# A fused field-interaction kernel on one core: later loads of F, a fifth output slot, and last-tile rows at 128 batches

## The chip, the cores and the metric

The kernel runs on one core of a Trainium2 chip. The metric is the device time of one launch in microseconds (us). Everything is float32 at the interface; the projections run on operands split into a high and a low part.

## The reference

```python
# F: (2048, 64, 128), W: (64, 64, 128), K_w and Q_w: (128, 128)
Kf  = einsum('bjd,ed->bje', F, K_w)
S   = einsum('bid,bjd->bij', F, Kf)
out = einsum('bij,ijd->bid', S, W) + einsum('bid,ed->bie', F, Q_w)
```

For every batch b a 64 x 64 table of scores S is made from F and its K projection. Each row i of that table is multiplied with its own 64 x 128 matrix W[i], and the Q projection of F is added.

## The kernel before, in words

The 2048 batches go in 16 tiles of 128 (`TILES`), a tile in 8 units of 16 batches (`UNITS`), and a tile's projection in 16 chunks of 512 columns (`CHUNKS`). F lies transposed in HBM. It comes in by pairs of units, 1 MB a load, into the six slots of `f_ring` (line 50), on the DMA queue of the sync engine (SP). One round of the steady state works on two tiles at once, and TensorE (PE) goes through it in this order (lines 514 to 518):

1. `scores_tile(t)` (L444, matmuls at L440): for each unit of tile t, 16 products of `kf` with F, into the unit's PSUM bank; `s_done` counts units. ACT and DVE copy the scores out in pairs of units into `s_t` (L217 to 219 and L314 to 316; `copy_s`). The banks are free of the earlier row sums when `out_done` says so (L454).
2. `project(t + 1)` (L406): for each chunk a K product (`k_done`) and a Q product (`q_done`), three matmuls each (L387 to 389): high by high, high by low, low by high. ACT copies both results out of PSUM (L199, L208). The high part `f_hi` of a unit is made by ACT (L194) or by DVE (L306), the low part `f_lo` by DVE (L292), both in three slots that come free with `q_done`. The first chunks each wait for the copies of the scores.
3. `rows_tile(t)` (L470, matmuls at L466): for each of 8 blocks, 4 values of m by 2 halves, W[i] against the scores of all 128 batches of the tile. Each block fills two banks; `o_done` counts blocks. DVE adds the Q part into an output slot of `o_sb` (L325, `sum_out`), counted by `out_done`, and SP stores the slot, 512 KB (L149, `store`). `sum_out` waits until the store from that slot four sums ago is done (L323). Blocks 4 to 7 wait for `out_done`, because they use the banks of blocks 0 to 3.

A float32 matmul stands as two instructions in the trace, each with its own weight load (LDWEIGHTS, shown as PEld). The split (fp32r) projection matmuls are one instruction each.

The order on SP is written out by hand (L160 to L172). In round t it is: stores 4 to 6 of tile t-1; the load of the first pair (`load_next(t, 0)`, L139) once two units of scores are made; store 7 of tile t-1; the loads of pairs 1, 2 and 3, once four, six and eight units of scores are made; and stores 0 to 3 of tile t. The pair that `load_next(t, j)` asks for has number 4t + j + 6 and overwrites the pair that the scores of units 2j and 2j+1 read last. So load 0 brings units 4 and 5 of tile t+1, load 1 its units 6 and 7, and loads 2 and 3 bring units 0 to 3 of tile t+2. With unit numbers counted over all tiles, DVE splits units 4, 6 and 8 (`both_f`) when the Q products of 4, 8 and 12 chunks of the projection are made (the wait at L305), and ACT splits 3, 5, 7 and 9 after chunks 1, 5, 9 and 13, and 10 at the round's end (L253 to L262).

The last tile has no projection behind its scores. Its rows go in another way (`rows_last`, L483): first for the batches of units 0 to 3 (part 0), then for those of units 4 to 7 (part 1), each in 4 blocks of 8 values of m with 64 batches (L504). DVE adds them with `sum_last` (L330, L338). So part 0 can begin while the scores of units 4 to 7 are still being copied.

Of the kernel before, what the change touches and what calls it, by code (L numbers as in the profile page):

```python
# [31 lines left out]
OBUF = 4  # L32
# [5 lines left out]
def build(nc, f_0, f_t, k_t, q_t, w, out):  # L38
    with ExitStack() as ctx:
# [21 lines left out]
        k_raw = sbuf("k_raw", [D, D])  # L61
        q_raw = sbuf("q_raw", [D, D])
# [4 lines left out]
        zeros = sbuf("zeros", [D, BANK], F32R)  # L67
# [19 lines left out]
        o_done, out_done = sem("o_done"), sem("out_done")  # L87
# [34 lines left out]

        lower, upper = slice(0, N), slice(N, P)
# [4 lines left out]
        def _(sp):  # L128
# [10 lines left out]
            def load_next(t, j):  # L139

                p = t * PAIRS + j + RING
                if p < TILES * PAIRS:
                    sp.wait_ge(s_done, t * UNITS + 2 * j + 2)
                    load_f(p)
# [15 lines left out]
            for t in range(TILES):  # L160
                if t >= 1:
                    for k in range(4, 7):
                        store(t - 1, k)
                load_next(t, 0)
                if t >= 1:
                    store(t - 1, 7)
                for j in range(1, PAIRS):
                    load_next(t, j)
                for k in range(4):
                    store(t, k)  # L170
            for k in range(4, UNITS):
                store(TILES - 1, k)  # L172
            for n in range(OBUF):
                sp.wait_ge(o_stored[n], 16 * (TILES * UNITS // OBUF))

        @block.scalar
        def _(act):
# [43 lines left out]
            act.dma_start(k_raw[:, :], k_t).then_inc(k_in, 16)  # L221
            act.dma_start(f_half_cols(1), f_0[0, :, half_cols(1)]).then_inc(f_half[1], 16)
            act.dma_start(q_raw[:, :], q_t).then_inc(q_in, 16)
            act.wait_ge(k_in, 16)
            nc.scalar.activation(k_hi[:, :], k_raw[:, :], COPY).then_inc(khi_done, 1)
# [3 lines left out]
            nc.scalar.activation(q_hi[:, :], q_raw[:, :], COPY).then_inc(qhi_done, 1)  # L229
# [33 lines left out]
            copy_s(TILES - 1, 1)  # L263
            copy_s(TILES - 1, 3)

        @block.vector
        def _(dve):
# [15 lines left out]
            def both_first(c):  # L283

                dve.wait_ge(f_first[c], 16)
                wait(dve, q_done, 2 * (c // 2 - SPLIT) + 2)
                nc.vector.tensor_copy(f_hi[:, c // 2 % SPLIT, piece_cols(c)], f_cols(c)).then_inc(fhi_dve, 1)
                dve.wait_ge(fhi_dve, c // 2)
                low_piece(c)
# [28 lines left out]
            def sum_out(t, k):  # L318
# [4 lines left out]
                wait(dve, o_stored[n % OBUF], n // OBUF * 16)  # L323
# [6 lines left out]
            def sum_last(half, k):  # L330

                n = (TILES - 1) * UNITS + half * 4 + k
                dve.wait_ge(o_done, n + 1)
                if half == 0 and k == 0:
                    dve.wait_ge(q_copied, TILES * CHUNKS)
                dve.wait_ge(o_stored[n % OBUF], n // OBUF * 16)
                bank = 2 * k % 8
                nc.vector.tensor_tensor(  # L338
                    o_sb[:, n % OBUF, :, :].rearrange("d s (x b) -> d s x b", b=KP * 4),
                    ps[:, bank:bank + 2, :].rearrange("d s (x b) -> d s x b", b=KP * 4),  # L340
                    q_out[:, (TILES - 1) % 2, :, :].rearrange("d (s m) (h b) -> d s (m h) b", s=2, h=2)[
                        :, :, k * 4 * IR:(k + 1) * 4 * IR, half * KP * 4:(half + 1) * KP * 4],
                    ALU.add).then_inc(out_done, 1)

            nc.vector.memset(zeros[:, :].bitcast(F32), 0.0).then_inc(zeros_done, 1)  # L345
            dve.wait_ge(khi_done, 1)
            nc.vector.tensor_tensor(k_lo[:, :], k_raw[:, :], k_hi[:, :].bitcast(F32),
# [4 lines left out]
            nc.vector.tensor_tensor(q_lo[:, :], q_raw[:, :], q_hi[:, :].bitcast(F32),  # L352
# [12 lines left out]
            for t in range(TILES):  # L365
# [11 lines left out]
                if t < TILES - 1:  # L377
                    for k in range(UNITS):
                        sum_out(t, k)
            for half in range(2):  # L380
                for k in range(4):
                    sum_last(half, k)

        @block.tensor
        def _(pe):
# [84 lines left out]
            def rows_tile(t):  # L470

                if t == 0:
                    pe.wait_ge(w_in, 16)
                for k in range(UNITS):
                    if k < 4:
# [3 lines left out]
                    else:  # L479
                        pe.wait_ge(out_done, t * UNITS + k - 3)  # L480
                    row_block(t, k)

            def rows_last(part):  # L483

                t = TILES - 1
                for k in range(4):
                    if part == 0:

                        pe.wait_ge(s_copied_act if k % 2 else s_copied, t * 2 + k // 2 + 1)
                        if k == 0:  # L490

                            pe.wait_ge(s_copied_act, t * 2 + 1)
                    else:
                        pe.wait_ge(out_done, t * UNITS + k + 1)
                    bank = 2 * k % 8
                    for x in range(2 * IR):
                        m = k * 2 * IR + x
                        for s in range(2):
                            half = slice(s * N, (s + 1) * N)
                            cols = s_t[half, m, :].rearrange("p (h b) -> p h b", h=2)[  # L500
# [49 lines left out]
```

## Time and profile before

| what | us |
|---|---|
| median of 3 runs | 623.38 |
| the runs | 621.13, 623.38, 625.32 |
| the profiled execution, its own time | 620.9 |
| its span, from the first to the last instruction | 619.1 |
| PE busy in the span | 606.5 (98%) |
| DVE busy | 403.9 |
| ACT busy | 402.0 |
| granted TensorE clock, mean | 0.995 |

The span is what the rows below are measured in. The other 1.8 us of the execution's own time lie around the span. In the rows, "PE" is the matmul, "PEld" its weight load, and "SPq" the sync engine as it issues DMAs. "Issue" as a releaser stands for idle time in which the engine waited for nothing that the profile shows.

### The profile page before, as it was taken

What the parts mean: (1) busy time and instruction counts of PE and PEld (TensorE: products, weight loads), DVE (VectorE), ACT (ScalarE), POOL (GpSimd) and SP (SyncE); (2) the same over time, 40 slices, a digit from 0 to 9 for tenths busy, and PEclk for the clock granted to TensorE, in tenths of its full rate; (3) what the DMA queues carried; (4) which work ended last, traced back from release to release, by engine and by line L of the source; (5) the groups of instructions that cost most, each with busy time, mean ns of one, the idle gap of its engine ahead of it and who ended that gap; (6) DMA issues with size and microseconds to landing.
All of it is one profiled execution on the core that took longest, in us unless ns stands there. A gap on an engine that the chain in (4) does not pass through costs nothing.

```text
span 619.1 us, 17442 instructions
## 1 busy us (share of the span) xinstructions
PE 606.5 (98%) x7822; PEld 535.9 (87%) x7822; DVE 403.9 (65%) x411; ACT 402.0 (65%) x695; POOL 0.2 (0%) x4
## 2 busy tenths in 40 slices
PE   9999999999999999899999999999989999999996
PEld 7888989889898988789889898898978889898896
DVE  6556758567595666657567686675946659476485
ACT  7887493866929387393874938669276592947720
POOL 0000000000000000000000000000000000000000
PEclk9999999999999999999999999999989999999999
DMA  8560937729185591935909367291852918646066
GB/s 327 233 266 35 372 140 262 284 105 373 68 299 247 199 343 48 373 130 210 336 34 357 156 245 300 103 369 76 309 236 98 375 74 292 255 163 247 4 271 274
DMA packets 29306, 137.57 MB, mean 222 GB/s; under 512 B 3248, under 2 KB 4016, under 8 KB 21168
## 3 DMA queue, kind: packets, MB, share of 16 engines
q1 hardware_dynamic: 28800, 136.20, 57.3%
q8 instruction: 62, 1.02, 0.6%
q10 hardware_dynamic: 432, 0.26, 0.1%
q14 instruction: 12, 0.10, 0.1%
HBM read 69.34 MB, written 67.11 MB: 220 GB/s over the span
## 4 chain that ended last, share of the span: by engine, by line
PE 94%; DMA 2%; DVE 1%; issue 1%; ACT 0%; DVEq 0%
PE ps L440 20%; PE ps L387 19%; PE ps L389 19%; PE ps L388 19%; PE ps L466 15%; PE ps L504 2%; DMA out<-o_sb 2%; DVE o_sb L325 1%; PE ps L511 1%; DVE o_sb L338 0%; ACT s_t L219 0%; ACT s_t L217 0%; DVE zeros L345 0%; ACT s_t L218 0%; DVEq L91 0%
## 5 line engine op out<-in xcount | busy, mean ns | idle before, releaser
L292 DVE TENSOR_TENSOR f_lo<-f_ring,f_hi 128x1024 fp32r<-128x1024 f32 x124 | 151.8, 1224 | 163.5 <-ACT f_hi L194 161.9
L208 ACT ACTIVATE q_out<-ps 128x512 f32<-128x512 f32 x256 | 156.7, 612 | 7.5 <-PE ps L389 0.3
L325 DVE TENSOR_TENSOR o_sb<-ps,q_out 128x1024 f32<-128x1024 f32 x120 | 140.2, 1219 | 32.5 <-PE ps L466 20.7
L199 ACT ACTIVATE kf<-ps 128x512 f32<-128x512 f32 x256 | 155.6, 608 | 7.8 <-PE ps L389 4.3
L217 ACT ACTIVATE s_t<-ps 128x512 f32<-128x512 f32 x32 | 19.1, 598 | 180.7 <-PE ps L440 180.7
L440 PE MATMUL ps<-f_ring,kf 128*64 128x64 f32 x4096 | 125.0, 223 | 1.7 <-issue 1.4
L440 PEld LDWEIGHTS ps<-f_ring,kf 128*64 128x64 f32 x4096 | 121.8, 138 | 5.0 <-issue 2.3
L466 PEld LDWEIGHTS ps<-s_t,w_sb 64*128 64x128 f32 x1920 | 108.4, 188 | 5.3 <-issue 5.3
L466 PE MATMUL ps<-s_t,w_sb 64*128 64x128 f32 x1920 | 111.2, 274 | 0.0
L387 PE MATMUL ps<-f_hi,k_hi 128*128 128x512 f32 (+1 forms) x258 | 102.0, 395 | 2.7 <-issue 2.7
L389 PE MATMUL ps<-f_hi,k_lo 128*128 128x512 f32 (+1 forms) x258 | 100.5, 390 | 1.9 <-issue 1.9
L388 PE MATMUL ps<-f_lo,k_hi 128*128 128x512 f32 (+1 forms) x258 | 100.5, 389 | 0.0
L387 PE MATMUL ps<-f_hi,q_hi 128*128 128x512 f32 x256 | 100.2, 391 | 0.0
L389 PE MATMUL ps<-f_hi,q_lo 128*128 128x512 f32 x256 | 99.9, 390 | 0.0
L388 PE MATMUL ps<-f_lo,q_hi 128*128 128x512 f32 x256 | 99.9, 390 | 0.0
L194 ACT ACTIVATE f_hi<-f_ring 128x1024 fp32r<-128x1024 f32 x77 | 82.0, 1064 | 0.0
L388 PEld LDWEIGHTS ps<-f_lo,k_hi 128*128 128x128 f32 x258 | 48.7, 189 | 12.5 <-issue 2.9
L387 PEld LDWEIGHTS ps<-f_hi,q_hi 128*128 128x128 f32 x256 | 48.3, 189 | 12.3 <-issue 2.1
L387 PEld LDWEIGHTS ps<-f_hi,k_hi 128*128 128x128 f32 x258 | 48.7, 189 | 10.6
L389 PEld LDWEIGHTS ps<-f_hi,k_lo 128*128 128x128 f32 x258 | 48.6, 189 | 10.1
L388 PEld LDWEIGHTS ps<-f_lo,q_hi 128*128 128x128 f32 x256 | 48.3, 189 | 10.1
L389 PEld LDWEIGHTS ps<-f_hi,q_lo 128*128 128x128 f32 x256 | 48.2, 188 | 10.2
(26 smaller groups left out, 195.3 us busy)
## 6 DMA issues: line engine op xcount, KB each, us to landing
out<-o_sb SPq DMA_DIRECT2D x128, 512.0 KB, 4.4
f_ring<-f_t SPq DMA_DIRECT2D x62, 1024.0 KB, 10.5
w_sb<-w SPq DMA_DIRECT2D x1, 2048.0 KB, 18.3
f_ring<-f SPq DMA_DIRECT2D x6, 256.0 KB, 4.7
f_ring<-f SPq DMA_DIRECT2D x3, 128.0 KB, 2.6
f_ring<-f ACTq DMA_DIRECT2D x1, 128.0 KB, 2.9
k_raw<-k_t ACTq DMA_DIRECT2D x1, 64.0 KB, 2.6
q_raw<-q_t ACTq DMA_DIRECT2D x1, 64.0 KB, 3.5
```

Source lines behind the costliest of these rows:

```text
L194: nc.scalar.activation(f_hi[:, v % SPLIT, :], f_unit(v), COPY).then_inc(fhi_done, 1)
L199: nc.scalar.activation(kf[:, c // 2, c % 2 * CK:(c % 2 + 1) * CK, :, :].rearrange("d k h i -> d (k h i)"), ps[:, 2 * c % 8, :], COPY).then ...
L208: nc.scalar.activation(q_out[:, t % 2, :, :].rearrange("d i (h b) -> d i h b", h=2)[:, :, :, at:at + CK], ps[:, (2 * c + 1) % 8, :].rearra ...
L217: nc.scalar.activation(s_t[:, :, same], src[:, 0, :, :], COPY)
L292: nc.vector.tensor_tensor(f_lo[:, v % SPLIT, :], f_unit(v), f_hi[:, v % SPLIT, :].bitcast(F32), ALU.subtract).then_inc(flo_done, 1)
L325: nc.vector.tensor_tensor(o_sb[:, n % OBUF, :, :], ps[:, bank:bank + 2, :], q_out[:, t % 2, :, :].rearrange("d (s m) b -> d s (m b)", s=2) ...
L387: nc.tensor.matmul(dst, w_hi[:, :], hi, start=True, stop=False)
L388: nc.tensor.matmul(dst, w_hi[:, :], lo, start=False, stop=False)
L389: return nc.tensor.matmul(dst, w_lo[:, :], hi, start=False, stop=True)
L440: ins = nc.tensor.matmul(ps[h * N:(h + 1) * N, e, k * N:(k + 1) * N], kf[:, e, k, h, :], rows, start=True, stop=True)
L466: ins = nc.tensor.matmul(ps[:, bank + s, x * P:(x + 1) * P], w_sb[half, m, :], cols, start=True, stop=True)
L504: ins = nc.tensor.matmul(ps[:, bank + s, x * N:(x + 1) * N], w_sb[half, m, :], cols, start=True, stop=True)
```

## The change

There are four parts. In each round the first load of F now waits for seven units of scores, and it comes after store 7 of the tile before. The other three loads also wait for K products of the next projection: chunks 2, 6 and 10 of it (`k_done` at 16(t+1) + 4j - 2). The output slots go from four to five. To make room, the raw K and Q weights move into `s_t`, which is not yet in use at the start, and the zeros of the warm-up move into slot 2 of `f_hi`, with one wait of DVE before that slot is first written. In the last tile the rows go as in the others, at 128 batches (L466). They begin when all scores have been copied; DVE copies those of units 0, 1 and 6 and ACT those of units 2 to 5 and 7. The first sum of the last tile and its store go in two halves of 256 KB. The host no longer unpacks the last tile in its own way.

```diff
@@ -29,7 +29,7 @@
...
 SPLIT = 3
-OBUF = 4
+OBUF = 5
 WARM = 8
@@ -58,13 +58,15 @@
...
         o_sb = sbuf("o_sb", [D, OBUF, 2, IR * P])
-        k_raw = sbuf("k_raw", [D, D])
-        q_raw = sbuf("q_raw", [D, D])
+        k_raw, q_raw = s_t[:, 0, :], s_t[:, 1, :]
         k_hi = sbuf("k_hi", [D, D], F32R)
...
         q_lo = sbuf("q_lo", [D, D], F32R)
-        zeros = sbuf("zeros", [D, BANK], F32R)
+        zeros = f_hi[:, 2, 0:BANK]
@@ -84,7 +86,7 @@
...
         s_done, s_copied, s_copied_act = sem("s_done"), sem("s_copied"), sem("s_copied_act")
-        o_done, out_done = sem("o_done"), sem("out_done")
+        o_done, out_done, out_half = sem("o_done"), sem("out_done"), sem("out_half")
         def wait(eng, semaphore, count):
@@ -119,6 +121,15 @@
...
             return slice(N + 2 * p * KP, N + 2 * (p + 1) * KP)
+        def scores_of_unit(e):
+            return ps[:, e, :].rearrange("p (k s m) -> p s m k", k=KP, s=2)
+        def same_unit(e):
+            return slice(e * KP, (e + 1) * KP)
+        def cross_unit(e):
+            return slice(N + e * KP, N + (e + 1) * KP)
         lower, upper = slice(0, N), slice(N, P)
@@ -138,9 +149,15 @@
...
                 if p < TILES * PAIRS:
-                    sp.wait_ge(s_done, t * UNITS + 2 * j + 2)
+                    if j == 0:
+                        sp.wait_ge(s_done, t * UNITS + 7)
+                    else:
+                        sp.wait_ge(s_done, t * UNITS + 2 * j + 2)
+                        sp.wait_ge(k_done, (t + 1) * CHUNKS + 4 * j - 2)
                     load_f(p)
@@ -159,19 +176,25 @@
...
                 if t >= 1:
-                    for k in range(4, 7):
+                    for k in range(4, UNITS):
                         store(t - 1, k)
-                load_next(t, 0)
-                if t >= 1:
-                    store(t - 1, 7)
-                for j in range(1, PAIRS):
+                for j in range(PAIRS):
                     load_next(t, j)
-                for k in range(4):
-                    store(t, k)
-            for k in range(4, UNITS):
-                store(TILES - 1, k)
+                if t < TILES - 1:
+                    for k in range(4):
+                        store(t, k)
+            t = TILES - 1
+            slot = t * UNITS % OBUF
+            sp.wait_ge(out_half, 1)
+            sp.dma_start(out[t, 0, :, 0:IR * P], o_sb[:, slot, 0, :]).then_inc(o_stored[slot], 16)
+            sp.wait_ge(out_done, t * UNITS + 1)
+            sp.dma_start(out[t, 0, :, IR * P:2 * IR * P], o_sb[:, slot, 1, :]).then_inc(o_stored[slot], 16)
+            for k in range(1, UNITS):
+                store(t, k)
             for n in range(OBUF):
-                sp.wait_ge(o_stored[n], 16 * (TILES * UNITS // OBUF))
+                uses = len(range(n, TILES * UNITS, OBUF)) + (1 if n == slot else 0)
+                sp.wait_ge(o_stored[n], 16 * uses)
         @block.scalar
@@ -218,15 +241,15 @@
...
                 nc.scalar.activation(s_t[lower, :, cross], src[upper, 1, :, :], COPY).then_inc(s_copied_act, 1)
-            act.dma_start(k_raw[:, :], k_t).then_inc(k_in, 16)
+            act.dma_start(k_raw, k_t).then_inc(k_in, 16)
             act.dma_start(f_half_cols(1), f_0[0, :, half_cols(1)]).then_inc(f_half[1], 16)
-            act.dma_start(q_raw[:, :], q_t).then_inc(q_in, 16)
+            act.dma_start(q_raw, q_t).then_inc(q_in, 16)
             act.wait_ge(k_in, 16)
-            nc.scalar.activation(k_hi[:, :], k_raw[:, :], COPY).then_inc(khi_done, 1)
+            nc.scalar.activation(k_hi[:, :], k_raw, COPY).then_inc(khi_done, 1)
             split_half(0)
...
             act.wait_ge(q_in, 16)
-            nc.scalar.activation(q_hi[:, :], q_raw[:, :], COPY).then_inc(qhi_done, 1)
+            nc.scalar.activation(q_hi[:, :], q_raw, COPY).then_inc(qhi_done, 1)
             split_half(2)
@@ -260,8 +283,15 @@
...
                 split_f((t + 1) * UNITS + 2)
-            copy_s(TILES - 1, 1)
-            copy_s(TILES - 1, 3)
+            t, e = TILES - 1, UNITS - 1
+            copy_s(t, 1)
+            copy_s(t, 2)
+            act.wait_ge(s_done, t * UNITS + e + 1)
+            src, same, cross = scores_of_unit(e), same_unit(e), cross_unit(e)
+            nc.scalar.activation(s_t[:, :, same], src[:, 0, :, :], COPY)
+            nc.scalar.activation(s_t[upper, :, cross], src[lower, 1, :, :], COPY)
+            nc.scalar.activation(s_t[lower, :, cross], src[upper, 1, :, :], COPY).then_inc(s_copied_act, 1)
         @block.vector
@@ -284,6 +314,9 @@
...
                 wait(dve, q_done, 2 * (c // 2 - SPLIT) + 2)
+                if c == 4:
+                    dve.wait_ge(k_done, 1)
                 nc.vector.tensor_copy(f_hi[:, c // 2 % SPLIT, piece_cols(c)], f_cols(c)).then_inc(fhi_dve, 1)
@@ -320,36 +353,32 @@
...
                     dve.wait_ge(q_copied, (t + 1) * CHUNKS)
-                wait(dve, o_stored[n % OBUF], n // OBUF * 16)
+                again = 1 if n - OBUF == (TILES - 1) * UNITS else 0
+                wait(dve, o_stored[n % OBUF], (n // OBUF + again) * 16)
                 bank = 2 * k % 8
...
                     ALU.add).then_inc(out_done, 1)
-            def sum_last(half, k):
-                n = (TILES - 1) * UNITS + half * 4 + k
-                dve.wait_ge(o_done, n + 1)
-                if half == 0 and k == 0:
-                    dve.wait_ge(q_copied, TILES * CHUNKS)
-                dve.wait_ge(o_stored[n % OBUF], n // OBUF * 16)
-                bank = 2 * k % 8
-                nc.vector.tensor_tensor(
-                    o_sb[:, n % OBUF, :, :].rearrange("d s (x b) -> d s x b", b=KP * 4),
-                    ps[:, bank:bank + 2, :].rearrange("d s (x b) -> d s x b", b=KP * 4),
-                    q_out[:, (TILES - 1) % 2, :, :].rearrange("d (s m) (h b) -> d s (m h) b", s=2, h=2)[
-                        :, :, k * 4 * IR:(k + 1) * 4 * IR, half * KP * 4:(half + 1) * KP * 4],
-                    ALU.add).then_inc(out_done, 1)
-            nc.vector.memset(zeros[:, :].bitcast(F32), 0.0).then_inc(zeros_done, 1)
+            def half_sum(k, half):
+                t, bank = TILES - 1, 2 * k % 8
+                n = t * UNITS + k
+                return nc.vector.tensor_tensor(
+                    o_sb[:, n % OBUF, half, :], ps[:, bank + half, :],
+                    q_out[:, t % 2, half * HALF + k * IR:half * HALF + (k + 1) * IR, :].rearrange("d m b -> d (m b)"),
+                    ALU.add)
+            nc.vector.memset(zeros.bitcast(F32), 0.0).then_inc(zeros_done, 1)
             dve.wait_ge(khi_done, 1)
-            nc.vector.tensor_tensor(k_lo[:, :], k_raw[:, :], k_hi[:, :].bitcast(F32),
+            nc.vector.tensor_tensor(k_lo[:, :], k_raw, k_hi[:, :].bitcast(F32),
                                     ALU.subtract).then_inc(klo_done, 1)
...
             dve.wait_ge(qhi_done, 1)
-            nc.vector.tensor_tensor(q_lo[:, :], q_raw[:, :], q_hi[:, :].bitcast(F32),
+            nc.vector.tensor_tensor(q_lo[:, :], q_raw, q_hi[:, :].bitcast(F32),
                                     ALU.subtract).then_inc(qlo_done, 1)
@@ -362,7 +391,7 @@
...
             low_f(9)
-            for t in range(TILES):
+            for t in range(TILES - 1):
                 v = (t + 1) * UNITS
@@ -374,12 +403,25 @@
...
                 low_f(v + 9)
-                if t < TILES - 1:
-                    for k in range(UNITS):
-                        sum_out(t, k)
-            for half in range(2):
-                for k in range(4):
-                    sum_last(half, k)
+                for k in range(UNITS):
+                    sum_out(t, k)
+            t = TILES - 1
+            copy_s(t, 0)
+            e = UNITS - 2
+            dve.wait_ge(s_done, t * UNITS + e + 1)
+            src, same, cross = scores_of_unit(e), same_unit(e), cross_unit(e)
+            nc.vector.tensor_copy(s_t[:, :, same], src[:, 0, :, :])
+            nc.vector.tensor_copy(s_t[upper, :, cross], src[lower, 1, :, :])
+            nc.vector.tensor_copy(s_t[lower, :, cross], src[upper, 1, :, :]).then_inc(s_copied, 1)
+            n = t * UNITS
+            dve.wait_ge(o_done, n + 1)
+            dve.wait_ge(q_copied, TILES * CHUNKS)
+            dve.wait_ge(o_stored[n % OBUF], n // OBUF * 16)
+            half_sum(0, 0).then_inc(out_half, 1)
+            half_sum(0, 1).then_inc(out_done, 1)
+            for k in range(1, UNITS):
+                sum_out(t, k)
         @block.tensor
@@ -471,53 +513,29 @@
...
                     pe.wait_ge(w_in, 16)
+                if t == TILES - 1:
+                    pe.wait_ge(s_copied, 2 * t + 2)
+                    pe.wait_ge(s_copied_act, 2 * t + 3)
                 for k in range(UNITS):
-                    if k < 4:
+                    if k >= 4:
+                        pe.wait_ge(out_done, t * UNITS + k - 3)
+                    elif t < TILES - 1:
                         pe.wait_ge(kf_copied, (t + 1) * CHUNKS + 13 + k)
                         pe.wait_ge(q_copied, (t + 1) * CHUNKS + 13 + k)
-                    else:
-                        pe.wait_ge(out_done, t * UNITS + k - 3)
                     row_block(t, k)
-            def rows_last(part):
-                t = TILES - 1
-                for k in range(4):
-                    if part == 0:
-                        pe.wait_ge(s_copied_act if k % 2 else s_copied, t * 2 + k // 2 + 1)
-                        if k == 0:
-                            pe.wait_ge(s_copied_act, t * 2 + 1)
-                    else:
-                        pe.wait_ge(out_done, t * UNITS + k + 1)
-                    bank = 2 * k % 8
-                    for x in range(2 * IR):
-                        m = k * 2 * IR + x
-                        for s in range(2):
-                            half = slice(s * N, (s + 1) * N)
-                            cols = s_t[half, m, :].rearrange("p (h b) -> p h b", h=2)[
-                                :, :, part * KP * 4:(part + 1) * KP * 4]
-                            if s:
-                                cols = cols[:, ::-1, :]
-                            ins = nc.tensor.matmul(ps[:, bank + s, x * N:(x + 1) * N], w_sb[half, m, :], cols,
-                                                   start=True, stop=True)
-                    ins.then_inc(o_done, 1)
             pe.wait_ge(zeros_done, 1)
             for n in range(WARM):
-                nc.tensor.matmul(ps[:, 0, :], zeros[:, :P], zeros[:, :], start=True, stop=True)
+                nc.tensor.matmul(ps[:, 0, :], zeros[:, 0:P], zeros, start=True, stop=True)
             pe.wait_ge(klo_done, 1)
...
                     project(t + 1)
-                    rows_tile(t)
-            for part in range(2):
-                rows_last(part)
+                rows_tile(t)
 def kernel(r_F, L0_rec_W, L0_rec_K_w, L0_rec_Q_w):
```

## Rows read from the trace of the kernel before

**Rows 1.** The page: queues, and the chain that ended last.

```profile
q1 hardware_dynamic: 28800, 136.20, 57.3%
q8 instruction: 62, 1.02, 0.6%
...
PE 94%; DMA 2%; DVE 1%; issue 1%; ACT 0%; DVEq 0%
```

**Rows 2.** Windows: an even round, four stretches with excess; us, busy (x), clock, DMA share, GB/s.

```profile
139.21:176.17 36.96, 36.96 (x482) 32.71 (x484) 24.91 (x25) 24.88 (x43) 0.00 (x0) 1.00 0.61 231
250.15:290.13 39.98, 37.26 (x482) 32.83 (x484) 25.03 (x26) 25.28 (x43) 0.00 (x0) 1.00 0.55 212
290.13:328.00 37.87, 37.23 (x482) 32.78 (x481) 24.64 (x26) 24.88 (x43) 0.00 (x0) 1.00 0.58 221
328.00:402.64 74.64, 74.56 (x962) 65.80 (x964) 50.67 (x51) 49.76 (x86) 0.00 (x0) 1.00 0.60 228
439.61:480.27 40.66, 38.79 (x482) 33.84 (x484) 25.05 (x26) 25.71 (x43) 0.00 (x0) 0.96 0.55 208
480.27:518.01 37.74, 37.20 (x480) 32.76 (x480) 24.64 (x26) 24.87 (x43) 0.00 (x0) 1.00 0.59 225
```

**Rows 3.** Windows: rows, scores and projection of one round; then a quiet stretch.

```profile
57.40:64.75 7.35, 7.35 (x131) 7.23 (x132) 6.33 (x7) 1.76 (x3) 0.00 (x0) 1.00 0.57 227
64.75:72.37 7.62, 7.62 (x257) 7.55 (x257) 5.83 (x7) 1.78 (x3) 0.00 (x0) 1.00 1.00 349
72.37:94.39 22.02, 22.02 (x98) 17.93 (x98) 12.83 (x14) 21.36 (x38) 0.00 (x0) 1.00 0.46 187
...
232.00:246.00 14.00, 14.00 (x106) 11.89 (x106) 8.36 (x9) 12.07 (x21) 0.00 (x0) 1.00 0.02 9
```

**Rows 4.** Timeline: PE's three kinds of gap; start, us, line, shapes, idle before.

```profile
262.23 0.39 PE L387 MATMUL ps<-f_hi,k_hi 128*128 128x512 f32 x1 [2.72 <-issue]
...
451.14 0.39 PE L389 MATMUL ps<-f_hi,k_lo 128*128 128x512 f32 x1 [1.87 <-issue]
...
295.48 3.02 PE L440 MATMUL ps<-f_ring,kf 128*64 128x64 f32 x95 [0.48 <-issue]
```

**Rows 5.** DMA queues in 252.6:259.7 (first row) and 259.7:262.3 (second).

```profile
q1 hardware_dynamic: 491, 2.31, 98.5%
...
q8 instruction: 1, 0.02, 2.2%
```

**Rows 6.** Timeline of SP's queue, one round (scores from 101.74).

```profile
103.95 1.27 SPq L136 DMA_DIRECT2D f_ring<-f_t  x1
...
106.66 3.57 SPq L136 DMA_DIRECT2D f_ring<-f_t  x3
```

**Rows 7.** The lines L136 (loads), then tile o_sb (stores): issue to landing, min/median/max.

```profile
DMA to landing us min/median/max: 6.1/10.5/13.9
...
DMA to landing us min/median/max: 2.7/4.4/10.6
```

**Rows 8.** The list of waits.

```profile
DVE o_sb L325 <- DMA out<-o_sb: 11.1, 10, 1.8
```

**Rows 9.** Timeline: the end of the last tile.

```profile
599.73 14.51 PE L504 MATMUL ps<-s_t,w_sb 64*128 64x64 f32 x256
599.85 0.60 ACT L217 ACTIVATE s_t<-ps 128x512 f32<-128x512 f32 x1 [1.93 <-PE ps L440]
...
614.29 1.23 DVE L338 TENSOR_TENSOR o_sb<-ps,q_out 128x1024 f32<-128x1024 f32 x1 [0.56 <-PE ps L504]
```

**Rows 10.** Lines by form: DVE at half length, the cast of a unit, ACT at 256 columns.

```profile
L275 DVE TENSOR_TENSOR f_lo<-f_ring,f_hi 128x512 fp32r<-128x512 f32 x6 | 4.2, 693 | 1.1 <-ACT f_hi L186 1.0
...
L306 DVE CAST f_hi<-f_ring 128x1024 fp32r<-128x1024 f32 x47 | 32.5, 692 | 1.6 <-PE ps L389 1.6
...
L180 ACT ACTIVATE f_hi<-f_ring 128x256 fp32r<-128x256 f32 x4 | 1.5, 405 | 0.0
```

**Rows 11.** Windows: PE after the gap that ends at 451.14.

```profile
451.14:456.00 4.86, 4.86 (x15) 3.82 (x15) 1.23 (x1) 3.34 (x6) 0.00 (x0) 0.65 1.02 428
```

More of the change, by code:

```diff
@@ L543 @@
     r = run_bass_kernel_spmd(nc, [arrays], core_ids=[0])
-    o = np.asarray(r.results[0]["out"])
-    o_most = o[:-1].reshape(TILES - 1, UNITS, D, 2, IR, 2, N).transpose(0, 6, 5, 3, 1, 4, 2).reshape(-1, N, D)
-    o_last = o[-1].reshape(2, 4, D, 2, 2 * IR, 2, N // 2).transpose(0, 6, 5, 3, 1, 4, 2).reshape(-1, N, D)
-    return np.ascontiguousarray(np.concatenate([o_most, o_last]))
+    o = np.asarray(r.results[0]["out"]).reshape(TILES, UNITS, D, 2, IR, 2, N)
+    return np.ascontiguousarray(o.transpose(0, 6, 5, 3, 1, 4, 2)).reshape(B, N, D)
```

## The prediction

> **What bounds the kernel now.** I read the page first. PE is busy 98% of the span and holds 94% of the chain that ended last [rows 1]. Another engine's speed matters only where it makes PE wait, so the question is how long PE works and where it stands still.
>
> Next I cut the span into rounds. An even round takes 36.96 us and PE is busy in all of it [rows 2]. It has 7.35 us of row sums, 7.62 of scores and 22.02 of projection [rows 3]. Some rounds are longer than that. Above 36.96 each (73.92 for the stretch of two), the other stretches of rows 2 cost 3.02, 0.91, 0.72, 3.70 and 0.78 us. That is 9.1 us, and it is nearly all that the middle of the kernel can give back.
>
> The timeline tells two kinds of excess apart. In the first PE stops "for issue", waiting for nothing the profile shows. There are two long gaps, 2.72 and 1.87 us, both 1 to 2 us into a projection, and three short ones in the middle of the scores, all under 0.5 us, of which one stands (0.48) [rows 4]. After the gap of 1.87 us the granted clock is 0.65 over 4.86 us [rows 11], which makes that round 3.70 us longer, not 1.87. In the second kind DVE's sum waits for the store that holds its output slot: 11.1 us in 10 waits, 1.8 at most [rows 8]. Most of that is slack, but some of it reaches PE through `out_done`.
>
> What does PE lack in the first kind? The page lists a queue "instruction" with 62 packets and 1.02 MB, so 16 KB a packet [rows 1]. For some 15,600 PE instructions that is about one packet in 255. Demand is uneven. The scores use 257 + 257 instructions in 7.62 us, or 67 per us, the row sums 131 + 132 in 7.35 (36 per us), and the projection 98 + 98 in 22.02 (9 per us) [rows 3]. A packet lasts under 4 us in the scores. Before the gap of 2.72 us the data queue fills the DMA engines to 98.5% for 7.1 us and no instruction packet passes. The next one comes after 259.7, and PE goes on at 262.23 [rows 4, 5]. In that stretch all four loads of the round are asked for: the first 2.2 us into the scores, the other three from 4.9 us on, in 3.57 us [rows 6]. Later in the round the DMA engines are empty: share 0.02 over 14 us [rows 3]. My reading is that a burst of 4 MB on the DMA engines makes the instruction packet late just when PE uses instructions fastest.
>
> **The later loads.** Nothing is added to the work; four loads per round move. Load 0 is now asked for after seven units (7 x 0.95 = 6.7 us into the scores). A chunk takes 22.02/16 = 1.38 us. Loads 1, 2 and 3 go after the K products of chunks 1, 5 and 9, so 2.1, 7.6 and 13.1 us into the projection. Behind the waiting load on SP are only the other loads and then store 0 of tile t, which is not due before the next rows. Store 7 no longer stands behind load 0.
> The gain: a packet asked for in the scores meets only stores. Both long gaps go, 3.02 + 3.70 = 6.7 us. Bounds: 0 if the gaps have another cause; 7.9 if the short ones go too. I keep the short gaps, because they come 4.7 to 5.0 us into the scores and a load had been in the queue for under 3 us by then; the stores filled it before. So -6.7.
> The cost, if the loads come too late: load 0 brings units 4 and 5 of the next tile. DVE may split them from 4 chunks on (5.5 us), and PE needs them at chunk 8 (11.0 us) less a cast, 0.69 [rows 10], and a low part, for which I take the 1.23 of a sum of the same size [rows 9], so by 9.1 us. The shortest landing of a load is 6.1 us [rows 7], which puts it at 6.7 + 6.1 - 7.62 = 5.2 us into the projection. That leaves 3.9 us. The other loads have 8.9 us each between asking and the first wish. With a transfer of 2.7 us each (57.3% of 619.1 us for 136.2 MB [rows 1]) and starts 5.5 us apart, they hardly meet. Cost 0.
>
> **Instruction fetch, rule and row.** The trace shows a gap that ends just after a late instruction packet [rows 4, 5]. The Trainium skill ("Runtime: NRT & Kernel Launch", section "Instruction fetch mechanics") says that 16 KB blocks of 256 instructions are fetched by the sequencer's own queue, and that this is mostly hidden. The size agrees with the 62 packets. By the second half of it the gaps would stay where they are, and this part of the change would be worth nothing; that is a rival below.
>
> **Five slots.** `sum_out` now waits for the store five sums back. A store lands in 4.4 us in the median [rows 7] and a sum takes 1.23 [rows 9]. Four slots give 3 x 1.23 = 3.7 us until the slot is wanted again, five give 4.9. So most of the 11.1 us goes. On PE's path it stands for what is left of the rounds' excess without the gaps: 0.91 - 0.48, then 0.72, then 0.78 - 0.48, together 1.45 us [rows 2, 4]. So -1.5. Bounds: 0 and -1.5.
> The price: SP may now have one more store queued when the scores begin, 1.37 us of transfer, and instruction packets wait behind stores as well. Today 3 of 15 rounds show a short gap of about 0.4 us. I allow for as many again, +1.2. Bounds: 0, and 12 more rounds at 0.48 = +5.8.
>
> **The last tile.** Today the 256 instructions of L504 take 14.51 us from 599.73 on [rows 9], 57 ns each with 64 batches. L466 takes 7.35/128, also 57 ns, with 128 batches [rows 3]. Half as many are needed, so the row sums fall to 7.35 us. But the end is not PE's. Step by step [rows 9, 10]:
> - PE now waits for the last unit's copy. ACT starts it at 599.85; three copies of half the length, by the 256-column form 0.405 each, end at 601.1. PE stands for 1.3 us. (Bounds per copy: 0.3 and 0.6.)
> - The first block takes 7.35/8 = 0.92, so 602.1 with the signal. Two half sums of 0.69: 603.5. Seven sums of 1.23: 612.1. PE is no longer the pace here; DVE is.
> - Today the last sum ends at 614.29 + 1.23 = 615.5 and the span at 619.1, so the last store and the end take 3.6 us. A store transfers in 1.37 us and a sum comes every 1.23, so seven stores fall behind by under 1 us; I take 0.2. End at 615.9.
> So -3.2. Bounds: -1 if the stores fall 2 us behind or PE's clock falls in its wait, -4 with copies of 0.3 us and no queue. Slots don't bind: sum 5 starts at about 608.4, when store 0, asked for by 603.5, has landed.
> The edits at the start cost nothing: the first K product is done before DVE comes to its third unit, and `s_t` is first written after the first scores.
>
> **The sum.** 619.1 - 6.7 - 1.5 + 1.2 - 3.2 = 608.9 of span; with the 1.8 around it 610.7 us. It is made against an execution of 620.9, which is 0.4% under the median of 623.38. The runs reach 625.32, and I think the difference is more gaps of the same kind. These would go as well, so I add nothing.
>
> **Rivals.**
> 1. The gaps aren't the loads' doing (the rule above). For: "issue" names no cause, and the first load of a round was asked for shortly before the short gaps too. Against: rows 5. Then 620.9 - 1.5 - 3.2 = 616.2. Chance 0.13.
> 2. The deeper store queue starves PE in the scores: 12 rounds more at 0.48. For: the three short gaps come out of stores. Against: sums and stores keep almost the same pace, so the queue seldom needs the fifth slot. 610.7 - 1.2 + 5.8 = 615.3. Chance 0.13.
> 3. On the other side: load 0 comes too late, and PE waits for `flo_done` at chunk 8 in each of the 15 rounds that have one. It decides from a landing of 9.1 + 7.62 - 6.7 = 10.0 us. For: today's median is 10.5 and the longest 13.9 [rows 7]. Against: these landed behind each other and behind stores [rows 6]. Now only the last stores lie ahead. At a landing of 12 us it costs 2.0 x 15 = 30, so 641. Slower than before by over 1% needs 11.3 us and more. Chance 0.04.
> 4. The later loads do nothing in the end because load 0, now over the start of the projection, makes the same long gaps at fewer rounds: half of 6.7 kept, 614.0. It stands within the range. Chance 0.06.
>
> **How the numbers follow.** The forecast, all three gains within 607 to 613.5, has 0.64. Range 607 to 617: it holds the forecast, rivals 1, 2 and 4 and the lower bound of all terms; the slower rival stays outside. A measurement of this kernel can tell about 1% from no change, so 617.1 and 629.6 are the borders. Faster by over 1%: the forecast 0.64, rival 2 and 4 nearly whole, 0.17, half of rival 1, 0.06, together 0.87. Within 1%: the rest of these, 0.09. Slower: 0.04.
>
> **What would show it.** Right: no round above 38 us; no "issue" gap over 1 us at the start of a projection; the waits of L325 for stores under 3 us in total; loads landing in 5 to 7 us in the median, and the DMA share lower in the scores and above 0.3 in the middle of the projection; in the last tile an idle PE of about 1.3 us, and sums back to back on DVE. Wrong: gaps as before (rival 1), short gaps in most rounds 4 to 6 us into the scores (rival 2), or PE at chunk 8 waiting for DVE with DVE waiting for a load (rival 3).

## The result, and the profile after

The changed kernel takes 617.47 us (median of 20 runs, 615.21 to 619.53); the kernel before takes 621.13 us beside it (20 runs, 617.28 to 625.89). The ratio is 0.9933 with a 95% interval of 0.9914 to 0.9953, so 2.9 to 5.3 us were won. The forecast was 610.7 and the range 607 to 617, so the time lies 0.5 us above the range. The profiled execution took 618.76 us with a span of 617.0.

The page of the changed kernel, queues, the chain by engine, and the DMA issues:

```profile
q1 hardware_dynamic: 28944, 136.20, 58.6%
q8 instruction: 61, 1.00, 0.6%
...
PE 96%; issue 1%; DVE 1%; DVEq 0%; ACT 0%; ACTq 0%
...
out<-o_sb SPq DMA_DIRECT2D x127, 512.0 KB, 4.8
f_ring<-f_t SPq DMA_DIRECT2D x62, 1024.0 KB, 4.9
```

PE is the bound as before [rows 1]. "DMA" is gone from the chain; in the kernel before it stood there for three sums in the middle of the kernel that waited for a store. A load now lands in 4.9 us in the median, where it took 10.5 [rows 7].

The list of waits (total us, times, longest):

```profile
PEld ps L482 <- issue: 7.4, 13, 0.9
...
PE ps L482 <- issue: 5.4, 12, 0.8
...
DVE o_sb L360 <- DMA out<-o_sb: 1.9, 4, 0.5
```

There is no gap at the start of a projection any more; in rows 4 two such gaps took 2.72 and 1.87 us. The sums wait 1.9 us for stores against 11.1 [rows 8]. But PE now stands "for issue" in the scores 12 times, 5.4 us together. The kernel before did so 4 times, for 1.4 us:

```profile
PE ps L440 <- issue: 1.4, 4, 0.5
```

Windows of whole rounds, and of a stretch in the middle of a projection:

```profile
101.72:139.51 37.79, 37.23 (x482) 32.84 (x484) 24.86 (x26) 24.89 (x43) 0.00 (x0) 1.00 0.59 223
214.57:252.00 37.43, 37.22 (x483) 32.85 (x484) 24.96 (x26) 24.87 (x43) 0.00 (x0) 1.00 0.60 226
252.00:288.96 36.96, 36.96 (x482) 32.72 (x484) 24.86 (x26) 24.87 (x43) 0.00 (x0) 1.00 0.61 229
326.69:364.70 38.01, 37.21 (x483) 32.84 (x484) 24.87 (x26) 24.86 (x43) 0.00 (x0) 1.00 0.61 225
...
232.00:246.00 14.00, 14.00 (x80) 11.56 (x80) 7.69 (x8) 13.51 (x24) 0.00 (x0) 1.00 0.39 147
```

The first four are whole rounds. An even round is still 36.96 us [rows 2], but 11 of the 15 rounds are 0.5 to 1 us longer, and each of these has one of the gaps; the twelfth, of 0.75 us, is in the last scores. A gap costs its round more than it lasts: PE also counts as busy for some 37.2 us there in place of 36.96. The share of 0.39 in the last row, 0.02 before [rows 3], is the loads in their new place.

The chain that ended last, in order of time:

```profile
27.81 7.62 PE ps L482 x256
...
106.53 0.56 issue
107.09 3.07 PE ps L482 x97
...
145.39 2.31 PE ps L482 x71
...
183.69 1.55 PE ps L482 x45
...
221.87 0.80 PE ps L482 x19
...
589.72 7.20 PE ps L482 x241
596.92 0.75 issue
597.67 0.70 PE ps L482 x15
```

The four rows from 107.09 to 221.87 each begin behind a short gap, with what is left of the scores: 97, 71, 45 and 19 matmuls. So from one gap to the next PE goes through a round and 26 matmuls more. A round has 256 + 128 + 96 matmuls with as many weight loads, 960 instructions; with 52 more these are 1012, and four instruction packets hold 4 x 252 = 1009 by the kernel before (15,644 PE instructions in 62 packets [rows 1]). The gaps keep step with the instruction packets. That doesn't say what makes a packet late.

From the first scores to the last scores' start the profiled execution takes 589.72 - 27.81 = 561.9 us. In the kernel before it was 592.19 - 27.31 = 564.9. The even rounds would be 15 x 36.96 = 554.4, so the excess fell from 10.5 to 7.5, by 3.0 and not to nothing. From the last scores' start to the end it is 617.0 - 589.7 = 27.3, against 26.9 before, where I had forecast 23.7.

### The profile page after: what moved, and what is told of

It reads as the page before. It is cut to its first block, busy times and chain, and to the rows that moved or that the text cites. A ratio compares the mean times of both kernels' runs of the same rounds, so it can differ in the third digit from the quotient of the medians.

```text
span 617.0 us, 17234 instructions
## 1 busy us (share of the span) xinstructions
PE 600.5 (97%) x7694; PEld 530.2 (86%) x7694; DVE 400.2 (65%) x412; ACT 401.8 (65%) x698; POOL 0.2 (0%) x4
## 4 chain that ended last, share of the span: by engine, by line
PE 96%; issue 1%; DVE 1%; DVEq 0%; ACT 0%; ACTq 0%
PE ps L482 20%; PE ps L429 19%; PE ps L430 19%; PE ps L431 19%; PE ps L508 18%; PE ps L531 1%; DVE o_sb L360 1%; DVEq L39 0%; DVE f_hi L374 0%; ACT s_t L294 0%; ACTq L39 0%; ACT s_t L292 0%; DVEq L93 0%
## 5 line engine op out<-in xcount | busy, mean ns | idle before, releaser
L360 DVE TENSOR_TENSOR o_sb<-ps,q_out 128x1024 f32<-128x1024 f32 x127 | 145.9, 1217 | 23.0 <-PE ps L508 21.1
L508 PEld LDWEIGHTS ps<-s_t,w_sb 64*128 64x128 f32 x2048 | 117.2, 190 | 6.7 <-issue 6.7
L508 PE MATMUL ps<-s_t,w_sb 64*128 64x128 f32 x2048 | 120.3, 276 | 1.3 <-ACT s_t L294 1.3
L429 PEld LDWEIGHTS ps<-f_hi,k_hi 128*128 128x128 f32 x258 | 48.7, 189 | 10.5
L429 PEld LDWEIGHTS ps<-f_hi,q_hi 128*128 128x128 f32 x256 | 48.1, 188 | 10.2 <-DVE q_lo L381 0.2
```

What stands on the lines that cost most here:

```text
L360: nc.vector.tensor_tensor(o_sb[:, n % OBUF, :, :], ps[:, bank:bank + 2, :], q_out[:, t % 2, :, :].rearrange("d (s m) b -> d s (m b)", s=2) ...
L429: nc.tensor.matmul(dst, w_hi[:, :], hi, start=True, stop=False)
L508: ins = nc.tensor.matmul(ps[:, bank + s, x * P:(x + 1) * P], w_sb[half, m, :], cols, start=True, stop=True)
```

## The experiments

"Short gaps" are the stops of PE for issue in the scores, nearly all under 1 us; the "long gaps" are the two of 2.72 and 1.87 us in rows 4. Two theories were set against each other first. A: instruction packets wait behind store data already asked for, and five slots leave more stores under way when the scores begin. B: the moved loads and the new order on SP make the short gaps. Theory C came after them. Each ratio below is to the kernel before, timed beside it, with its 95% interval.

**One part at a time.** `loads_only`, in the kernel before:

```diff
-                    sp.wait_ge(s_done, t * UNITS + 2 * j + 2)
+                    if j == 0:
+                        sp.wait_ge(s_done, t * UNITS + 7)
+                    else:
+                        sp.wait_ge(s_done, t * UNITS + 2 * j + 2)
+                        sp.wait_ge(k_done, (t + 1) * CHUNKS + 4 * j - 2)
...
-                    for k in range(4, 7):
+                    for k in range(4, UNITS):
```

> The kernel before with only the later loads (and store 7 ahead of load 0); four slots, old last tile. Theory A (instruction packets wait behind whatever data is queued; five slots deepen the queue of stores when the scores begin): no gap over 1 us, three to five short ones as before, DVE still waiting about 8 to 11 us for stores; about 6 us faster than before. Theory B (the short gaps of the changed kernel come from the moved loads and the new order on SP, not from the slots): short gaps of 0.4 to 0.8 us in 10 or more of 16 rounds here too; at most 3 us faster.

`slots_only`, in the kernel before, with the scratch tiles moved as in the change:

```diff
-OBUF = 4
+OBUF = 5
```

> The kernel before with five slots (and the scratch tiles moved to make room), loads and last tile as before. Theory A: short gaps in 10 or more rounds, long gaps stay or grow, waits of the sums for stores fall to about 2 us in total; 0 to 5 us slower than before. Theory B: gaps as before, 1 us faster at most.

`tail_only`: the changed kernel with `OBUF = 4` and the loads and their order on SP put back.

> The kernel before with the new last tile alone (four slots; the scratch tiles stay moved). Both theories: PE stands for about 1.4 us before the last row sums, the granted clock falls to about 0.56 for some 3.5 us, the stores then run one behind the other at about 395 GB/s; from the start of the last scores to the end 26 to 27.5 us against 26.91 before, so within 1 us of the kernel before. If the clock doesn't fall here, that stretch takes about 26.

`after_4slots`, in the changed kernel:

```diff
-OBUF = 5
+OBUF = 4
```

> The changed kernel with four slots in place of five. Theory A: the short gaps fall from 13 rounds to 3 to 6, the sums wait 8 us and more for stores; 1 to 3 us faster than the changed kernel. Theory B: short gaps as in the changed kernel, and 1 to 2 us slower than it because the waits for slots come back.

| kernel | median us | ratio | interval |
|---|---|---|---|
| later loads only | 616.06 | 0.9911 | 0.9883 to 0.9940 |
| five slots only | 625.84 | 1.0055 | 1.0028 to 1.0081 |
| last tile only | 618.76 | 0.9947 | 0.9928 to 0.9966 |
| changed, four slots | 613.73 | 0.9870 | 0.9842 to 0.9898 |

The waits of the later loads alone, of the five slots alone, and of the changed kernel with four slots:

```profile
DVE o_sb L326 <- DMA out<-o_sb: 13.7, 11, 2.2
...
PE ps L441 <- issue: 2.3, 5, 0.6
```

```profile
PE ps L441 <- issue: 4.2, 10, 0.6
...
PE ps L388 <- issue: 2.7, 1, 2.7
...
PE ps L390 <- issue: 1.8, 1, 1.8
...
DVE o_sb L326 <- DMA out<-o_sb: 0.8, 2, 0.5
```

```profile
DVE o_sb L360 <- DMA out<-o_sb: 15.9, 13, 2.0
...
PE ps L482 <- issue: 1.9, 4, 0.6
```

Theory B falls. The moved loads take the long gaps away and leave the short ones at 5. Five slots alone bring 10 short gaps, keep both long ones, and make the kernel slower, although the sums hardly wait for stores any more. Taken out of the changed kernel, the fifth slot gives 3.7 us back (613.73 for 617.47, the ratios 0.9870 and 0.9933 with intervals apart): the edit saved 14 us of waits that were nearly all slack, and paid in gaps that aren't. In the two profiled executions the rounds account for 1.8 us of the difference and the stretch from the last scores on for 2.4; what happens there comes below. `tail_only` did not come as expected: it was 2.1 to 4.5 us faster and not within 1 us, and in its profile the granted clock didn't fall.

**Are the stores what delays PE?** `half_bytes`, in the changed kernel; it leaves half of the output unwritten (but for the last tile's first block), and its rows are half as long:

```diff
-                sp.dma_start(out[t, k, :, :],
-                             o_sb[:, n % OBUF, :, :].rearrange("d s n -> d (s n)")).then_inc(o_stored[n % OBUF], 16)
+                sp.dma_start(out[t, k, :, 0:IR * P],
+                             o_sb[:, n % OBUF, 0, :]).then_inc(o_stored[n % OBUF], 16)
```

> The changed kernel with only the first half of each output slot stored (256 KB of 512), except in the last tile's first block: half of the output is left out. Theories A and C: no gap over 0.3 us in the scores, rounds all within 0.2 us of 36.96, and about 7 us less in the rounds; the last tile shorter too. If the gaps stay, stores have nothing to do with them.

It took 605.96 us, ratio 0.9744 (0.9705 to 0.9782). A window of one round, and the only waits of the scores for issue:

```profile
212.00:249.00 37.00, 37.00 (x486) 32.74 (x486) 24.89 (x26) 24.88 (x43) 0.00 (x0) 1.00 0.49 172
```

```profile
PEld ps L482 <- issue: 0.4, 1, 0.4
```

With half the bytes PE doesn't stand at all in the round shown, though it runs the same instructions; the one wait left in the scores, 0.4 us, is of a weight load. The short gaps are the stores' doing. Whether the bytes or the shorter rows take them away, this run can't tell.

**What in the stores?** Theory C says that a packet waits behind a fixed number of descriptors (the pieces in which a DMA's bytes are asked for) while the data queue isn't empty. `under_way_4` and `under_way_3` limit the stores under way in the changed kernel (here 4; the other has 3):

```diff
                 sp.wait_ge(out_done, n + 1)
+                if 4 <= n < (TILES - 1) * UNITS:
+                    sp.wait_ge(o_stored[(n - 4) % OBUF], 16 * ((n - 4) // OBUF + 1))
```

> The changed kernel (five slots), but SP asks for a store only when the store four before it has landed, outside the last tile. Theory A (an instruction packet waits behind all the store data that has been asked for and not moved yet, so the number of stores under way is what counts, not the number of slots): short gaps fall to about 6 as with four slots, the sums hardly wait for stores, the same or 1 us faster than the changed kernel with four slots (613.7): 612 to 615. Theory C (the packet waits behind a fixed number of descriptors as long as the queue is not empty): gaps nearly as in the changed kernel, 616 to 618.

> The same with three stores under way at most. Theory A: 0 to 3 short gaps in the scores, 610 to 613 us, as the stores still end before the next loads. Theory C: gaps only where the queue stays full, so some fewer than in the changed kernel, 614 to 617. Loss in both if the stores come so late that the sums wait for slots (over 5 us of such waits in the profile).

`two_dmas` halves the rows, with the waits on `o_stored` at twice the count:

```diff
-                sp.dma_start(out[t, k, :, :],
-                             o_sb[:, n % OBUF, :, :].rearrange("d s n -> d (s n)")).then_inc(o_stored[n % OBUF], 16)
+                for s in range(2):
+                    sp.dma_start(out[t, k, :, s * IR * P:(s + 1) * IR * P],
+                                 o_sb[:, n % OBUF, s, :]).then_inc(o_stored[n % OBUF], 16)
```

> The changed kernel with each store asked for as two DMAs of 256 KB, rows of 2048 bytes in place of 4096: same bytes, twice the descriptors, 8% more transfer time by the packets' durations of 0.086 against 0.159 us. Theory A: gaps as in the changed kernel or slightly longer, 617 to 620. Theory C: the wait behind a fixed number of descriptors is half as long, short gaps gone, 609 to 612.

`two_dmas_4slots` is the same with `OBUF = 4`. `two_dmas_loads` also splits each steady load into its two units. `before_short_rows` has both splits in the kernel before.

> The changed kernel with split stores (2048-byte rows) and four slots in place of five. Theory C alone: the number of slots hardly matters once the rows are short, and the waits for slots come back, so 612 to 614 against 612.05 with five. If the number of stores under way adds to the delay as well: 610.5 to 611.5.

> The changed kernel with split stores, and the steady loads of F split by unit too (4096-byte rows). In the changed kernel the loads come where PE uses few instructions, so both theories: the same as with split stores alone within 1 us, 611 to 613.

> The kernel before (old schedule of the loads, four slots, old last tile), only with every store and every steady load of F asked for as two DMAs with rows half as long (2048 and 4096 bytes). Theory C (an instruction packet waits behind a fixed number of descriptors): the long gaps shrink to under 1 us or vanish without any load being moved, short gaps gone; 613 to 616 us. If the packet waits behind bytes that have been asked for (theory A), both kinds stay: 620 to 624.

`short_rows_3` and `short_rows_2` are `two_dmas_loads` with three or two stores under way.

> The changed kernel with stores and loads split into two DMAs of half the row length, and three stores under way at most outside the last tile. If row length and the number of stores under way both delay the instruction packets, their effects add: short gaps gone, rounds' excess under 1 us in all, 609 to 610.5 us. If row length alone counts (theory C), the limit brings nothing: 610.5 to 612, against 610.89 without it.

> The same with two stores under way. Theory A+C: no gap left, but the last stores of a tile are late; the sums wait for slots for over 5 us in total, some of it on PE, and load 0 goes out later: 610 to 613. If the gaps come from stores under way alone and the stores still keep up, 609 to 610.

| kernel | median us | ratio | interval |
|---|---|---|---|
| changed, 4 under way | 616.45 | 0.9912 | 0.9884 to 0.9940 |
| changed, 3 under way | 612.82 | 0.9852 | 0.9819 to 0.9885 |
| changed, split stores | 612.05 | 0.9833 | 0.9799 to 0.9867 |
| the same, four slots | 614.72 | 0.9904 | 0.9872 to 0.9936 |
| changed, split stores and loads | 610.89 | 0.9849 | 0.9816 to 0.9881 |
| before, split stores and loads | 618.51 | 0.9962 | 0.9936 to 0.9987 |
| split, 3 under way | 611.40 | 0.9837 | 0.9810 to 0.9866 |
| split, 2 under way | 612.61 | 0.9862 | 0.9833 to 0.9891 |

The waits with four and with three stores under way, then with split stores and five slots, then with split stores and four:

```profile
PE ps L484 <- issue: 3.3, 5, 1.0
```

```profile
DVE o_sb L362 <- DMA out<-o_sb: 2.5, 5, 0.7
...
PE ps L484 <- issue: 2.3, 5, 0.6
```

```profile
DVE o_sb L360 <- DMA out<-o_sb: 3.4, 7, 0.7
...
PE ps L482 <- issue: 0.5, 2, 0.3
```

```profile
DVE o_sb L360 <- DMA out<-o_sb: 20.7, 24, 2.1
```

Both answers have a part. Three under way in place of up to five brings the short gaps from 12 to 5, with the same rows. Half rows bring them to 2, with the same bytes and five slots. With split stores four slots are worse than five: the gaps are gone there too, so the waits for slots (20.7 us) are what is left, and some of them reach PE. From the first to the last scores' start that kernel's profile has 4.5 us over even rounds, against 1.7 with five slots. Once both effects are small, they don't add: all variants with split stores and five slots lie between 610.9 and 612.6, and their intervals overlap. The time of `under_way_4` can't be told from the changed kernel's, although its profile has only 5 gaps, as with three under way; for 5 gaps I had expected 612 to 615 us, and why it took 616.45 is open. With two under way another wait comes up, for loads of F, which now go out later behind the stores:

```profile
DVE f_hi L343 <- DMA f_ring<-f_t: 29.0, 16, 4.5
```

In the kernel before, the split alone won only 0.4%. Gaps of over 1 us stayed, one in the scores and one in a projection; the waits there read:

```profile
DVE o_sb L327 <- DMA out<-o_sb: 19.9, 20, 2.2
...
PE ps L442 <- issue: 1.6, 2, 1.4
...
PE ps L391 <- issue: 1.1, 1, 1.1
```

So short rows don't replace the later loads. Theory C in its pure form is wrong too: it gave 613 to 616 us for this kernel and 614 to 617 for `under_way_3`. What isn't separated is row length from the mere fact of two DMAs; no kernel had long rows in twice as many DMAs. Nor does any run show how a late packet and the stores meet in the queues; that the packet waits behind the stores is my reading.

**The last tile.** `after_filled`, in the changed kernel:

```diff
                 if t == TILES - 1:
+                    pe.wait_ge(s_copied, 2 * t + 1)
+                    for n in range(6):
+                        nc.tensor.matmul(ps[:, 0, :], k_hi[:, :], f_hi[:, 0, 0:BANK], start=True, stop=True)
                     pe.wait_ge(s_copied, 2 * t + 2)
```

> The changed kernel with six more matmuls of 512 columns on PE between the last scores and the last row sums, into a bank that is free by then; their results are not used. If the last tile's loss over the forecast comes from the granted clock (0.56 over the first 3.5 us of the row sums after PE stood still twice), the clock stays at 1.00, the stretch from the last scores to the end falls from 27.3 to 25 or 26 us, and the kernel gets 1 to 1.5 us faster, 616 to 616.5. If the loss is in the queue of stores, the stretch stays above 27.

Timelines of PE: the changed kernel, the same with four slots, and with the filling matmuls; behind the first, windows of the changed kernel:

```profile
599.70 9.04 PE L508 MATMUL ps<-s_t,w_sb 64*128 64x128 f32 x128 [1.34 <-ACT s_t L294]
```

```profile
597.40:599.70 2.30, 0.69 (x16) 0.58 (x16) 0.34 (x1) 1.14 (x3) 0.00 (x0) 1.00 0.02 7
599.70:603.20 3.50, 3.50 (x36) 3.50 (x38) 1.29 (x2) 0.00 (x0) 0.00 (x0) 0.56 0.07 22
...
608.70:611.20 2.50, 0.04 (x2) 0.00 (x0) 2.50 (x3) 0.00 (x0) 0.00 (x0) 1.00 1.00 395
611.20:617.00 5.80, 0.00 (x0) 0.00 (x0) 0.01 (x1) 0.00 (x0) 0.00 (x0) 0.72 0.57 225
```

```profile
596.49 7.42 PE L508 MATMUL ps<-s_t,w_sb 64*128 64x128 f32 x128 [1.35 <-ACT s_t L294]
```

```profile
596.86 0.68 PE L482 MATMUL ps<-f_ring,kf 128*64 128x64 f32 x15 [0.75 <-issue]
597.47 1.66 PE L519 MATMUL ps<-f_hi,k_hi 128*128 128x512 f32 x6
599.06 7.42 PE L508 MATMUL ps<-s_t,w_sb 64*128 64x128 f32 x128
```

In the changed kernel PE stood 0.75 us for issue and then 1.34 for ACT. After that the granted clock was 0.56 for 3.5 us (nearly all of it at 1.2 of 2.4 GHz) and the row sums took 9.04 us. With four slots PE stood for ACT as long but not for issue before it, and the clock held: 7.42 us. With the filling it had the same gap for issue, 0.75, yet the clock held. Ten other profiled kernels with the new last tile have the wait of 1.34 or 1.35 us without a gap in the last scores, and in all of them the row sums took 7.42 us. From the last scores' start to the end this stretch took 27.3 us in the changed kernel, and 615.1 - 588.9 = 26.2 with the filling, where the last scores start at 588.90 by the chain. The kernel's ratio is 0.9926 (0.9903 to 0.9949), which overlaps the changed kernel's: some 1.1 us show in the profile, which is too small for the timing; 1 to 1.5 us faster was expected. How many of the timed executions had the fall is not known.

## Why the prediction was wrong

**The step that failed** is "Five slots". I put it at -1.45 for the waits and +1.2 for new gaps, so near nothing. Alone it costs 0.55% (0.28 to 0.81), some 3.4 us of 621. The bound of +5.8 had held it, and rival 2 told the mechanism, more short gaps from stores, and its sign came: a gap in most rounds, 4.8 to 7.3 us into the scores. It had 12 more of them; there are 12 in all, 8 more than before. My reason against it, that sums and stores keep almost the same pace so that the queue seldom needs the fifth slot, was the error. In the kernel before the sums waited 10 times for a store to land; each of these waits was a place where the fifth slot would be used, and those rows stood before me [rows 8]. By my reading the waits also held the stores back, and so let PE's instruction packets through. I valued the wait at what it cost and not at what it protected. The -1.45 was too large as well. I took all that was left of a round's excess beside its gap for waits on PE's path; but in the changed kernel, where no sum's wait reaches PE, a round with a gap has such a rest too, some 0.27 us of longer PE work, and rows 2 show the same 37.2 for 36.96. About 0.5 of the 1.45 was the gaps' own, and a new gap was to be priced at about 0.7 us, not 0.4.

**Later loads.** Forecast -6.7. Alone the ratio is 0.9911 (0.9883 to 0.9940), 3.7 to 7.3 us; in its profile the excess of the rounds fell from 10.5 to 5.5 us. Both long gaps are gone, and load 0 is in time: all loads land in 4.9 us in the median, where rival 3 needed over 10, and no engine's wait for them is in the list of the changed kernel. Right in kind, and somewhat less than the 6.7: 5.5 us by the ratio. The short gaps were not the loads' and stayed, as the step said.

**The rule in the Trainium skill** ("Runtime: NRT & Kernel Launch", section "Instruction fetch mechanics") calls the fetch mostly hidden. Rival 1 rested on it and falls: with half the stored bytes the gaps of 5.4 us vanish, and with the loads moved those of 2.72 and 1.87 us. Here the fetch is not hidden when the data queue fills the DMA engines (98.5% before the gap of 2.72 us [rows 5]). The 616.2 of rival 1 left out the +1.2 of the stores that the forecast has; with it, it is 617.4.

**The last tile.** Forecast -3.2. Alone the ratio is 0.9947 (0.9928 to 0.9966), 2.1 to 4.5 us: right as a part. Its profile has 617.0 - 592.2 = 24.8 us from the last scores' start on, against 26.9, so 2.1 of the 3.2. In the profiled execution of the changed kernel it gave nothing, 27.3 us for the forecast 23.7. Row sums begin 9.98 us after the last scores' start for 8.9 in the forecast, 0.75 of it the gap for issue. The first sum began at 601.50, 1.8 us after the row sums, at the low clock. The last sum ended at 611.2 and the span 5.8 us later, not 3.8: at 395 GB/s the stores come one behind the other, and the queue that I took as 0.2 us was 2.2, a little over my bound. My own sum for it, seven stores at 1.37 us behind sums at 1.23, already gave nearly 1. The copies were as forecast, three of 0.38 to 0.39 us.

**The sum.** The three parts alone multiply to 0.9911 x 1.0055 x 0.9947 = 0.9913, and 0.9933 was measured; with the intervals of the three factors the two agree. Forecast for the kernel: -10.2 us. It was short by 3.7 us through the slots (613.73 without the fifth, still 3 above the forecast); the rest can be read in the profile of the four-slot kernel. Its scores start at 27.42 and 587.52, so its excess is 560.1 - 554.4 = 5.7 us where my terms left 10.5 - 6.7 - 1.45 + 1.2 = 3.5 (my rows of excess had added up to 9.1; 1.4 us lay in rounds that I didn't count), and from the last scores' start to the end it takes 612.4 - 587.5 = 24.9 where I had 23.7. The execution that I started from (620.9) is near the median of 20 runs (621.13), so the base was sound; my guess that its median stood higher for more gaps was not needed.

## What to carry to other kernels

A buffer more was not free here, where stores follow each other closely: the waits that it removed were mostly slack, while more stores under way brought more gaps for issue. When PE stands "for issue" in its densest stretch, look at what data is queued then: move bulk loads to where PE uses few instructions, limit the transfers under way, or ask for them in shorter rows. The fastest kernels here keep the five slots and split the stores (610.9 to 612.6 us against 617.5); three stores under way without the split came as near as can be told (612.8).

## What had not been expected of the hardware

- Asking for 512 KB as two DMAs with rows of 2048 bytes in place of one with 4096 made the gaps for issue fall from 5.4 to 0.5 us at the same number of bytes (612.05 us, 617.47 before the split).
- One wait of 1.35 us left the granted clock at 1.00; one of 0.75 and, 0.7 us of scores later, one of 1.34 were followed by 0.56 for 3.5 us. The gap of 2.72 us in rows 4 was followed by no such fall (1.00 from 262.23 to 270 us) and that of 1.87 was, by 0.65 over 4.86 us [rows 11].
